# Moving one basis unit behind the first output projection, and the first root weight's load behind the transposes

## The reference

```python
h = relu(layernorm(x)); x = x + L0(h)   # attention over the graph, 8 heads, then a feed-forward layer
h = relu(layernorm(x)); x = x + L1(h)   # linear + prelu, then twice: (h + A h), two linears, batch norm, relu
h = relu(layernorm(x)); x = x + L2(h)   # graph convolution: D^-1/2 A D^-1/2 (h W) + b, leaky relu
h = relu(layernorm(x)); x = x + L3(h)   # two relational layers

# L0: softmax over the heads' query index, masked by the adjacency matrix
scores = einsum('nhd,mhd->nhm', q, k) / 8; attn = softmax(where(adj, scores, -1e9), axis=1)
out = einsum('nhm,mhd->nhd', attn, v) @ Wo + bo
# L3, each of its two layers, r in (0, 1)
w[r] = einsum('b,bio->io', att[r], basis)          # 30 basis matrices of 512 x 512
out = segment_sum(gate * x[col] @ w[type]) + x @ root + bias
```

## Time and profile before

| | us |
|---|---|
| median of 3 runs | 455.6 (455.17 to 456.53) |
| the profiled execution, whole time | 459.73 |
| its span | 457.9 |
| TensorE busy | 441.6 |
| VectorE busy | 346.4 |
| ScalarE busy | 243.6 |
| mean transfer rate over the span | 217 GB/s |

### The profile page before, as it was taken

One profiled execution on the slowest core, in us unless ns is written; L12 is line 12 of the kernel. 1 busy time (PEld: TensorE's weight loads), 2 busy tenths in 40 slices (PEclk: granted clock), 3 DMA queues, 4 the chain that ended last, 5 costly groups with the idle time before them and its releaser, 6 DMA issues.

```text
span 457.9 us, 6200 instructions
## 1 busy us (share of the span) xinstructions
PE 441.6 (96%) x2226; PEld 275.4 (60%) x2226; DVE 346.4 (76%) x736; ACT 243.6 (53%) x428; POOL 42.7 (9%) x59
## 2 busy tenths in 40 slices
PE   8999999899997999999999999999989999999997
PEld 3334453444432345768756867677357688888885
DVE  5999996899999849785879675766778695866212
ACT  5999994676897516562246335535662523511210
POOL 3240000024224002000010000010000000000000
PEclk9999999999999799999999999999999999999999
DMA  7997348426699747979089856687871740000002
GB/s 258 414 392 170 115 167 324 160 92 233 245 374 353 278 192 250 424 263 383 36 336 342 318 213 285 247 320 284 318 250 49 290 178 16 1 0 2 0 3 92
DMA packets 18090, 99.22 MB, mean 217 GB/s; under 512 B 2959, under 2 KB 3599, under 8 KB 7567
## 3 DMA queue, kind: packets, MB, share of 16 engines
q1 hardware_dynamic: 13191, 72.72, 42.4%
q0 software_dynamic: 4000, 25.18, 14.9%
q10 hardware_dynamic: 864, 0.86, 0.6%
HBM read 93.50 MB, written 5.25 MB: 216 GB/s over the span
## 4 chain that ended last, share of the span: by engine, by line
PE 72%; DVE 14%; DMA 10%; issue 2%; ACT 1%; DVEq 0%; SPq 0%
PE bank L1371 20%; PE sbank L1703 10%; DMA bring<-in_basis 7%; PE bank L1716 6%; PE sbank L1357 6%; PE sbank L1427 6%; PE sbank L1567 4%; PE bank L1688 4%; PE bank L1450 3%; PE bank L1357 3%; PE bank L1411 2%; DVE stat L853 2%; PE sbank L1411 2%; DMA wring<-in_weights 2%; PE bank L1513 2%; PE sbank L1490 2%
## 5 line engine op out<-in xcount | busy, mean ns | idle before, releaser
L1357 PE MATMUL sbank<-bring,attw 120*32 120x512 f32 x336 | 41.0, 599 | 2.2 <-DMA bring<-in_basis 2.2
L839 DVE TENSOR_SCALAR cnt<-iota_row,edge_f 128x512 bf16<-128x512 f16 x132 | 41.2, 347 | 0.4 <-PE sbank L1427 0.4
L466 ACT ACTIVATE stat<-stat,eps 128x1 f32<-128x1 f32 x32 | 9.4, 294 | 42.9 <-DVE stat L858 42.9
L1427 PE MATMUL sbank<-cnt,adjT 128*128 128x512 bf16 x132 | 30.6, 380 | 0.3
L576 ACT ACTIVATE adjT<-distance,edge_w,edge_f 128x128 bf16<-128x128 bf16 x61 | 29.3, 480 | 1.4 <-PE sbank L1427 1.4
L1281 DVE SCALAR_TENSOR_TENSOR y_lo<-sbank,gate,y_hi 128x512 fp32r<-128x512 f32 x16 | 11.8, 750 | 22.6 <-ACT y_hi L765 22.5
L497 ACT ACTIVATE s<-bank,colsb 128x512 f32<-128x512 f32 x24 | 16.4, 687 | 21.8 <-PE bank L1371 21.8
L1427 PEld LDWEIGHTS sbank<-cnt,adjT 128*128 128x128 bf16 x132 | 12.3, 98 | 21.7 <-DVE cnt L839 6.4
L1371 PE MATMUL bank<-hT_hi,w_hi 128*128 128x512 f32 x64 | 25.3, 395 | 0.0
L529 ACT ACTIVATE distance<-iota_row,edge_f 128x128 bf16<-128x128 f16 x61 | 24.3, 400 | 1.8 <-DVE edge_f L905 0.4
L1371 PE MATMUL bank<-hT_hi,w_lo 128*128 128x512 f32 x64 | 24.9, 390 | 0.0
(11 more groups left out here) (250 smaller groups left out, 1095.9 us busy)
## 6 DMA issues: line engine op xcount, KB each, us to landing
bring<-in_basis SPq DMA_DIRECT2D x59, 1024.0 KB, 9.7
wring<-in_weights POOLq DMA_DIRECT2D x8, 1024.0 KB, 10.0
landing<-in_weights POOLq DMA_DIRECT2D x4, 1024.0 KB, 5.1
w_scratch<-stage SPq DMA_DIRECT2D x16, 256.0 KB
hT<-in_weights POOLq DMA_DIRECT2D x4, 1024.0 KB, 8.4
qkw<-w_scratch POOLq DMA_DIRECT2D x2, 2048.0 KB, 8.0
rring<-in_rows POOLq DMA_DIRECT2D x12, 256.0 KB, 8.3
wring<-in_basis SPq DMA_DIRECT2D x2, 1024.0 KB, 12.9
```

The lines of the kernel that those rows point to most:

```text
L839: dve.tensor_scalar(hot_s[:, n % HOT, :], iota[:, :], src_f[:, n:n + 1], None, ALU.is_equal).then_inc(sem("hot_ready"), 1)
L1357: mm = pe.matmul(unit_bank(b)[32 * j:32 * j + 32, :], attw[0:KB, u // UNITS, g, :], unit_place(u)[0:KB, j, :], start=(g == 0), stop=(g == ...
L1427: pe.matmul(bank[7][:, :], hot_d[:, n % HOT, :], hot_s[:, n % HOT, :], start=(n == 0), stop=(n == ECH - 1)).then_inc(sem("hot_used"), 1)
```

## The change

`STEP_UNITS` gives the units of the eight steps. Step 5, the sixth, has two instead of three; step 7, the last, has one instead of none. In step 7 the units are now called between `project(0)` and `attend(6)`; in the other steps they stay at the end. The sum is 18 as before, so the units behind the loop keep their numbers. In `LAST_READ` the load of root1 now waits for `x4_psum` instead of `c2_1_psum`.

```diff
-STEP_UNITS = (1, 2, 3, 3, 3, 3, 3, 0)
+STEP_UNITS = (1, 2, 3, 3, 3, 2, 3, 1)
...
-             "root1": ("c2_1_psum", C), "root2": ("c2_1_psum", C)}
+             "root1": ("x4_psum", C), "root2": ("c2_1_psum", C)}
...
                     if it == 2 * C - 1:
                         project(0)
+                        units(STEP_UNITS[it])
                     if it:
                         attend(it - 1)
...
-                    units(STEP_UNITS[it])
+                    if it < 2 * C - 1:
+                        units(STEP_UNITS[it])
```

## The result

| | before | changed |
|---|---|---|
| median of the runs, us | 456.06 (5 runs, 455.17 to 456.7) | 458.5 (5 runs, 458.48 to 459.37) |
| ratio, with its 95% interval | | 1.006 (1.0043 to 1.0077) |
| the profiled execution, us | 459.73 | 458.48 |
| its span, us | 457.9 | 456.7 |

The changed kernel is slower by 0.6%, 2.4 us. The forecast was 1.1 us faster, 454.5, with a range that ended at 456.3: the prediction was wrong, and on the wrong side. The two profiled executions alone would say the opposite, 1.3 us faster. That is the first thing to take apart.

What follows compares the result with a forecast made beforehand. TensorE bounds the kernel (busy 441.6 of 457.9 us), stopping for ring loads at the two places changed. From the median: 455.6 - 0 (unit order) - 1.1 (root1's load) = 454.5 us, range 451.0 to 456.3.

Steps and rivals of the forecast that it cites:

- Edit 1, the steps: End of the attention: reordered units remove unit 25's wait of 1.31 us; `project(2)` starts at 162.76 instead of 165.75.
- Edit 1, the value: End of the attention: 3.0 us gained if timed runs have the clock's fall, otherwise 0; 0 was taken.
- Rival A: Attention: the clock's fall is in the timed runs too, so the change gains 4.1 us, to 451.5; chance 0.22.
- Rival B: Before `project(2)`: a stop of 1.66 us brings a new clock fall costing 3.4 us, to 457.9; chance 0.09.
- Edit 2, the landing of unit 60: After the last batch norm: unit 60's load lands at 332.1, 5.0 us after unit 59's; bounds 327.0 and 334.5.
- Edit 2, the lump: After the last batch norm: unit 59's wait of 0.90 us goes, and TensorE wants unit 60 at 332.5.
- rival C: After the last batch norm: root1's later load holds up unit 60 or 61, the wait only moves: 455.6; chance 0.12.
- The cap on edit 2: Last 8 aggregation matmuls: VectorE's fourth part lets at most 1.29 of 2.19 us be kept; the term is 1.1.
- Rival D: Last aggregation matmuls: VectorE's fourth part sets no limit on the gain from moving root1: 453.4; chance 0.07.

Runs made afterwards that it cites:

- e1: The kernel before with only the new unit order, root1's load waiting as before: 456.29 us against 456.32, ratio 1.0002.
- e2: The kernel before with only root1's load changed to wait for `x4_psum`, old unit order: 459.45 us against 456.32, ratio 1.0075.
- e12: The kernel before, old unit order, with root1's load waiting until unit 59 has been used: 455.28 us against 456.22, ratio 0.998.
- e13: Repeat of e9 with more rounds (changed kernel, root1's load waiting until unit 59 has been used): 455.23 us against 456.22, ratio 0.9974.
- e11: Repeat of e6 with more rounds (changed kernel, store of batch 12 behind unit 60's load): 455.17 us against 456.48, ratio 0.9969.
- e4: The changed kernel with ten short matmuls, whose results are not read, put before unit 60: 457.02 us against 456.32 before, ratio 1.0016.
- e5: The changed kernel without root1's load, its splits reading the gcn weight instead: 454.88 us against 456.33 before, ratio 0.996.
- e10: The changed kernel itself, run again unaltered: 458.4 us against 456.48 before, ratio 1.0055.
- e6: The changed kernel with the 256 KB store of batch 12 issued behind unit 60's load: 455.12 us against 456.33 before, ratio 0.9969.
- e7: The kernel before with the 256 KB store of batch 12 issued behind unit 60's load: 456.02 us against 456.33, ratio 0.9987.
- e9: The changed kernel with root1's load waiting until unit 59 has been used: 454.28 us against 456.48 before, ratio 0.9954.

## Why the prediction was wrong, point by point

**Edit 1, the steps: right.** Forecast and measured, in us on the time axis of the profiles: `project(0)` 148.0 and 147.71; end of the second projection 158.2 and 157.91; TensorE free 161.1 and 160.78; VectorE's second take 159.75 and 159.46; `project(2)` 162.76 and 162.43. That the saved wait goes into a longer one before `project(2)` is right too: 1.65 us after 160.78, where 1.66 was forecast. Only unit 24 waited less than the 1.3 us of the forecast: 0.96, and 0.50 to 1.08 in the nine profiles with this order.

**Edit 1, the value: right.** "Without the fall of the clock edit 1 is worth nothing" came out in e1 (1.0002), in e2's row at 162.66, and in e12 against e13. The choice that hung on it, to take the fall in the profile for that of one execution and not of the median, was right. A fall of 6.84 us at half clock leaves a mean of 0.993. Of 110 executions of the kernel before, four are at 0.992 or 0.993, the profiled one at 0.993. Rival A, which is about the median, is excluded. But the fall is not confined to that profile. The profile of e12, with the old order, has a shorter one at the same place (unit 25, `project(0)`), at a mean clock of 0.995:

```profile
149.36 1.93 PE L1357 MATMUL bank<-bring,attw 120*32 120x512 f32 x8 [1.29 <-DMA bring<-in_basis]
151.22 4.36 PE L1567 MATMUL sbank<-wring,qkw 128*128 128x512 f32 x8
```

`project(2)` starts at 164.14 there, 1.5 us later than in e2. So two of the five profiles of the old order have a fall in the attention, and none of the nine of the new order has one there. Low executions, without the kernels that have the gathered stop of edit 2 unfilled, are 41 of 144 with the old order and 11 of 73 with the new, over several chips and variants. Edit 1 may thus take some falls out of the mean; no run was made to show it.

**Rival B, a fall before `project(2)`: came in one profile, not in the median.** In the profile of the changed kernel the stop of 1.65 us is there, with a clock of 1.00 before it and 7.13 us for the two projections behind it. The profile of e11, with the same unit order, has a stop of 2.00 us at this place and the fall behind it (row of the timeline, then the window):

```profile
162.43 8.83 PE L1568 MATMUL sbank<-wring,qkw 128*128 128x512 f32 x16 [2.00 <-ACT qkw L622]
```
```profile
162.43:165.80 3.37, 3.37 (x4) 1.41 (x5) 0.31 (x1) 0.00 (x0) 0.00 (x0) 0.52 1.01 428
```

The two projections take 1.7 us more there; the rival had 3.4. The other eight profiles with this order show no fall there, although two of them have stops of 2.12 (e4) and 2.11 us (e13). The rival's mechanism, a stop gathered into one piece and then a fall, is thus real at the place that it named, in one profile of nine, and it is also what made the kernel slower at a place that it did not name.

**Edit 2, the landing of unit 60: the step that failed.** The prediction took the 5.0 us between the landings of units 59 and 60 as the time that unit 60 needs, and put it behind a landing of unit 59 that comes earlier: 332.1 on the axis of before. The measured distance is (319.65 + 12.1) - (318.73 + 5.5) = 7.5 us. The 5.0 was a distance behind a root1 that had already landed (321.06 + 5.2 = 326.3); it is 5.0 again in e5, where root1's load is left out. In the profile of before root1 went through first. The queue of the profile before that moved data in 322.5 to 325.2, with packets, MB and share of the 16 engines:

```profile
q0 software_dynamic: 107, 0.88, 84.1%
```

Here q0 is the queue of GpSimd's loads. The view has no row for q1, the queue of the ring loads: in this stretch they got nothing, although unit 59's load had been issued at 321.82. In the changed kernel the same queue moved its first packets within 1 us of the issue of unit 59's load. Its rows for 323.5 to 327 and then 327 to 331:

```profile
q1 hardware_dynamic: 237, 0.99, 73.2%
q0 software_dynamic: 33, 0.27, 22.3%
```
```profile
q1 hardware_dynamic: 124, 0.97, 57.5%
q0 software_dynamic: 100, 0.75, 44.4%
```

Until unit 60 is there, the same bytes must be moved in both kernels: unit 59's, the store's, unit 60's and root1's. Only who is served first has changed, and unit 60, the last of these ring loads, gains nothing by that. It lands 0.4 (changed kernel) to 0.9 us (e10) later than before, against the start of the section. The Trainium skill ("DMA: Bandwidth & Descriptors", Queues, rings and completion order), as the prediction cited it, has the engines go round-robin between the queues. The 57.5 and 44.4% agree; the 322.5 to 325.2 of before, where one queue had it all, don't show it. The prediction used the rule to move unit 60 by 0.9 us, to "near 333". On that axis it landed at 331.77 + (320.70 - 317.60) = 334.87, beyond the bound of 334.5.

**Edit 2, the lump.** That unit 59 would no longer wait was right, and so TensorE reaches unit 60's wait 0.90 earlier. But this wait was not shorter for it: 0.90 + 1.29 became one of 2.56 to 3.10. This is rival C ("the wait only moves"), with chance 0.12. It was priced at 455.6, at no loss, and that was the second error. A wait that is gathered into one piece was taken to cost what its parts had cost. Its own cost is the 1.46 us of low clock in the section. 20 of 21 executions were low; the fall was seen behind this stop in two of the three that were profiled. The stretch of the attention in which 1.31 us behind 1.03 had been followed by a fall stood in the prediction, and rival B used it; the same question was not put at unit 60, although the bound of 334.5 for its landing gave a stop of 2.2 us or more there.

**The sum, as measured.** The later landing costs 0.4 to 0.9, the fall 1.5, together 1.8 (changed kernel) to 2.2 (e2) in the section, against a median 2.4 and 3.1 above that of before. The low executions of before (median 457.59, against 456.24 for those that are not low) are in its median too, so the whole difference is not accounted for to the last half microsecond, and stays so.

**The cap on edit 2: right.** e5, e6, e7, e9, e11, e12 and e13 have a section of 19.50 to 19.53, and 20.59 - 1.08 was the forecast's 1.1. In all seven the last eight matmuls wait 0.3 to 0.7 us for VectorE's fourth part. Rival D is excluded: even with unit 60's wait at zero nothing more comes. The edit was aimed at a real 1.1 us; it takes another place of root1's load to get it.

**What stays open.** Where in the timed executions of before the low clock lies isn't known; they give only a mean. The profiles of before and of e12 show it in the attention. Whether e2's larger loss against the changed kernel's (1.0075 and 1.006, with overlapping intervals) is the unit order or chance wasn't settled. That 256 KB of store cost the load of 1 MB behind it 2.1 us with root1 in front and 4.1 or more with root1 behind was measured in one or two profiles each, but not explained.

## What to carry to other kernels

A load that is moved back is not gone: before you move one, list everything that must land until the last wait behind it, and ask whether that sum has changed; if not, only the order in which you wait has. Price a wait that gathers two short ones for the clock too: here the fall behind it cost more (1.5 us) than the wait itself had grown (0.4 to 0.9). Where a load is the bound, look at what small transfers stand in front of it in its own queue; moving one store of 256 KB, or the other load until this one was nearly through, gave the whole 1.1 us in the section.

## What was not expected of the hardware

- A stop of 3.10 us was not followed by a fall (e10, profiled execution), one of 2.56 was. Before `project(2)` one of 2.00 was (e11), those of 2.11 and 2.12 (e13, e4) were not. In the attention 1.03 and 1.31 us with one unit between them (before), and 1.19 and 1.29 (e12), were; 0.98 and 1.31 (e7), and 0.81 and 1.31 (e2), were not. The changed kernel was low in 9 of 10 executions (e10). The Trainium skill ("TensorE: Matmul & The Clock Gate", Part 1) calls the window in which TensorE's activity is watched free-running; that one program gives both results agrees with it. A stop raises the chance of a fall rather than deciding it.
- Ten short matmuls on zeros (2.33 us) in a stop brought the low executions from 9 of 10 to 1 of 10.
- A store of 256 KB cost the load of 1 MB behind it 4.1 us (12.1 against 8.0) with root1's load issued after both (6.6 instead of 8.0 in the repeat e11), and 2.1 us (11.7 against 9.6) with root1's in front.
- A load of 1 MB on GpSimd's queue, issued before the ring loads, took 84% of the 16 engines' time for 2.7 us, in which the ring loads' queue moved nothing; issued behind one ring load, it took 22 and then 44%.
